# Centring the output weights on chip, one residual update per tile, and the attention denominator as a ninth place of the state product, in a two-layer transformer block with top-1 experts

## What is computed

```
x = x + layernorm(attention(layernorm(x)))
x = x + layernorm(ffn(layernorm(x)))

attention: q, k, v = x @ W + b;  16 heads of 8;  q, k = elu(q) + 1, elu(k) + 1
  s = running sum of k v^T over the tokens of a sequence;  z = running sum of k
  value = (q s) / (q z + 1e-6);  output = values @ Wo + bo
ffn: logits = x @ w_router.T;  the best of 16 experts per token, score = sigmoid(logit)
  out = (silu(x w_gate.T) * (x w_up.T)) @ w_down.T
      + (up * silu(gate)) @ down_proj of the chosen expert, on score * x
layernorm(y) = (y - mean(y)) / sqrt(var(y) + 1e-5), no gain, no offset
```

## Time and profile before

| | |
|---|---|
| time of 3 runs | 351.54 us median, 349.24 to 351.72 |
| the profiled execution | 347.56 us, its span 345.8 us |
| busy, share of the span | PE 264.6 us (77%), DVE 286.4 us (83%), ACT 186.6 us (54%), POOL 192.7 us (56%) |
| granted TensorE clock, mean | 0.913 of 2.4 GHz |
| stage 1 | up to about 154 us of the span |
| stage 2 | up to about 230 us |
| stage 3 | from about 240 us, its last PE product before 325 us |

### The profile page before, as it was taken

How to read it: one execution, slowest core, us unless ns; L and a number is a source line. 1 busy time by engine, 2 the same in 40 slices (tenths; PEclk the granted TensorE clock), 3 DMA queues, 4 the chain that set the end, 5 groups by cost and what they waited for, 6 DMA issues and landing times.

```text
span 345.8 us, 6250 instructions
## 1 busy us (share of the span) xinstructions
PE 264.6 (77%) x1465; PEld 184.2 (53%) x1465; DVE 286.4 (83%) x1138; ACT 186.6 (54%) x572; POOL 192.7 (56%) x221
## 2 busy tenths in 40 slices
PE   3459999999998995638887988821999999999000
PEld 1125556555554553325555655521999889988000
DVE  5998999999999999996998787640379999999930
ACT  2524656565665552257666664203899888885000
POOL 5056777767775863200054556570007888888870
PEclk9988999999999998967999899985899999999655
DMA  6999900000000000000011111126950101110000
GB/s 187 374 426 396 396 4 0 2 3 0 2 0 2 2 0 0 1 1 2 1 62 64 63 62 64 64 100 229 355 166 18 35 31 43 41 36 29 25 2 0
DMA packets 13668, 28.39 MB, mean 82 GB/s; under 512 B 1950, under 2 KB 10150, under 8 KB 12610
## 3 DMA queue, kind: packets, MB, share of 16 engines
q1 hardware_dynamic: 10448, 21.57, 17.1%
q0 software_dynamic: 3040, 6.37, 5.4%
q10 hardware_dynamic: 146, 0.07, 0.1%
HBM read 15.38 MB, written 13.60 MB: 84 GB/s over the span
## 4 chain that ended last, share of the span: by engine, by line
PE 39%; DVE 24%; POOL 18%; issue 12%; DMA 4%; ACT 1%; POOLq 0%; ACTq 0%; SPq 0%; another core or an unknown queue 0%; DVEq 0%
PE banks L1009 13%; POOL out L490 10%; POOL rows L484 6%; PE banks L1028 5%; PE banks L1100 5%; DVE hT L814 2%; PE banks L1037 2%; PE banks L1134 2%; POOL sorted_rows L474 2%; DVE stats L641 2%; DMA rows<-in_x 2%; PE banks L997 2%; DVE num L740 1%; DVE rows L857 1%; DVE stats L849 1%
## 5 line engine op out<-in xcount | busy, mean ns | idle before, releaser
L1009 PE MATMUL banks<-kv,upto 128*128 128x512 f32 x128 | 63.5, 621 | 1.3 <-POOL kv L449 1.3
L449 POOL TENSOR_TENSOR kv<-qk,vv 128x1024 f32<-128x1024 f32 x32 | 62.4, 1950 | 2.5
L1134 PE MATMUL banks<-xsT,w_now 128*128 128x128 f32 x376 | 52.6, 284 | 0.4 <-DVE hT_e L948 0.4
L490 POOL DMA_INDIRECT out<-rows,token_i x47 | 46.8, 997 | 9.8 <-issue 8.2
L443 POOL TENSOR_TENSOR qk<-ex,rl 128x256 f32<-128x256 f32 x32 | 23.3, 727 | 47.0 <-ACT ex L546 47.0
L1134 PEld LDWEIGHTS banks<-xsT,w_now 128*128 128x128 f32 x376 | 47.1, 197 | 1.2 <-issue 0.7
L474 POOL DMA_INDIRECT sorted_rows<-rows,slot_i x32 | 31.7, 992 | 28.7 <-DVE slot_i L804 20.7
L718 DVE TENSOR_TENSOR prod<-banks,qk 128x1024 f32<-128x1024 f32 x32 | 38.9, 1216 | 2.1 <-PE banks L1009 1.5
L740 DVE TENSOR_REDUCE num<-prod 128x128 f32<-128x1024 f32 x32 | 38.7, 1208 | 0.3 <-DVE den L735 0.3
L948 DVE TENSOR_TENSOR hT_e<-silu_e,banks 128x256 f32<-128x256 f32 x47 | 19.4, 412 | 19.8 <-ACT silu_e L623 16.1
L484 POOL TENSOR_TENSOR rows<-rows,yn 128x128 f32<-128x128 f32 x40 | 19.1, 477 | 28.0 <-DVE yn L940 26.1
(11 more groups left out here) (158 smaller groups left out, 640.0 us busy)
## 6 DMA issues: line engine op xcount, KB each, us to landing
sorted_rows<-rows SPq DMA_DIRECT2D x3, 1950.0 KB, 13.3
rows<-sorted_rows SPq DMA_DIRECT2D x11, 520.0 KB, 6.3
w_exp<-in_gate_up SPq DMA_DIRECT2D x4, 1024.0 KB, 19.7
w_exp_down<-in_down SPq DMA_DIRECT2D x4, 512.0 KB, 19.7
rows<-in_x SPq DMA_DIRECT2D x1, 1024.0 KB, 11.1
rows<-in_x SPq DMA_DIRECT2D x1, 768.0 KB, 8.4
out<-rows,token_i POOLq DMA_INDIRECT x47
sorted_rows<-rows,slot_i POOLq DMA_INDIRECT x32
```

Of the source, the lines that this page charges most:

```text
L449: nc.gpsimd.tensor_tensor(kv[:, u, :].rearrange("p (h m d) -> p h m d", h=NH, m=HD), k, v, ALU.mult).then_inc(s_kv, 1)
L490: nc.gpsimd.indirect_dma_start(out=out_rows, out_offset=bass.IndirectOffsetOnAxis(ap=token_i[:, j - 1:j], axis=0), in_=rows[:, j - 1, 0:D] ...
L1009: ins = nc.tensor.matmul(ps_s[u % 2][:, cols], upto[:], kv[:, u, cols], start=True, stop=True)
L1134: ins = nc.tensor.matmul(ps_gue[u % 2][:, c * P:(c + 1) * P], w_now[:, u % 2, c * P:(c + 1) * P], xsT[:, u % 2, :], start=True, stop=True)
```

## The change

Two things are done together.

*Centring.* The last step of both sub-layers is linear, so a mean over the 128 outputs can be taken out of the weights: DVE subtracts from each row of Wo, of the shared w_down, of every expert's down_proj and of bo its mean (`centre_steps`: a sum of the row, then one fused instruction). Then the layernorm of the output needs no offset: x + y * rstd is one fused DVE instruction per tile. In stage 2 ACT's `ya` and DVE's two adds per group go, and four fused instructions come. In stage 3 `yn`, POOL's add and DVE's last adds go, and the norm steps of a quad are 12 in place of 15 (`scale_steps`, 11, which uses that the two half means are opposite, and the token index); the output of tile i is made one quad after its sum, in place of two, and POOL only sends. Wo and bo are centred before the first statistics, w_down in tile 4 of stage 1, the experts' weights after the routing is done.

*Ninth place.* The attention output is laid out place first (the weights are permuted on the host), so that k stands behind the eight products k v of each tile in one array `kvq`, and the sum of k (128 columns) lands right behind the 1024 columns of the state in PSUM. DVE makes one product of 1152 columns and one reduction to 144 values, in place of two of each. PE sums k after the state and not before it, and waits first until v of the next tile has been read. ACT adds epsilon in even tiles. The projection is written to the other parity's banks, and waits for the product of the tile before. In odd tiles DVE adds the carried parts afterwards.

```diff
+def centre_steps(nc, series, rows_of, sums, ready=None):
+    n, width = rows_of.shape[1], rows_of.shape[2]
+    yield series.done(nc.vector.tensor_reduce(sums, rows_of, AX, ALU.add))
+    series.wait()
+    ins = nc.vector.scalar_tensor_tensor(
+        out=rows_of, in0=sums.rearrange("p (n o) -> p n o", o=1).to_broadcast([P, n, width]), scalar=-1.0 / width,
+        in1=rows_of, op0=ALU.mult, op1=ALU.add)
+    yield ins.then_inc(ready, 1) if ready else ins
...
+            for j in range(ST):
+                pool.wait_ge(s_fin, j + 1)
+                nc.gpsimd.indirect_dma_start(
+                    out=out_rows, out_offset=bass.IndirectOffsetOnAxis(ap=token_i[:, j:j + 1], axis=0),
+                    in_=rows[:, j, 0:D], in_offset=None,
+                    bounds_check=NTOK - 1, oob_is_err=False).then_inc(s_out, 16)
...
+                if u % 2 and live(t - 1, NT):
+                    if t == 1:
+                        act.wait_ge(s_eps, 1)
+                    act.wait_ge(s_sums, t)
+                    nc.scalar.activation(den[:, 0, :], sums[:, 0, D:CW], ACT.Identity, bias=eps_den[:]).then_inc(s_den, 1)
...
-                if live(s + 3, NG):
-                    act.wait_ge(s_norm2, s + 4)
-                    for k in range(GT):
-                        c = tiles(GT * (s + 3) + k)
-                        ins = nc.scalar.activation(
-                            ya[:, (u + 1) % 2, k * D:(k + 1) * D], flat(rows[:, c, D:2 * D]),
...
+            centring = Series(dve, s_centre, 0)
+            dve.wait_ge(s_bias, 16)
+            finish(centre_steps(nc, centring, bias[:].rearrange("p (n d) -> p n d", n=1), row_sums[:, 0:1])
+                   ).then_inc(s_centred_o, 1)
+            dve.wait_ge(s_w, 16)
...
-                    dve.wait_ge(s_z, t + 1)
-                    nc.vector.tensor_tensor(zq[:], ps_qkv[u % 2][:, 3 * D:4 * D], qk[:, u, 0:D],
-                                            ALU.mult).then_inc(s_chain, 1)
+                    dve.wait_ge(s_s, t + 1)
+                    at_least(dve, s_sums, t - 1)
+                    nc.vector.tensor_tensor(
+                        prod[:, u % 2, :].rearrange("p (m c) -> p m c", c=D),
+                        ps_s[u % 2].rearrange("p (m c) -> p m c", c=D),
+                        kvq[:, u, Q0:Q0 + D].rearrange("p (o c) -> p o c", o=1).to_broadcast([P, HD + 1, D]),
+                        ALU.mult).then_inc(s_prod, 1)
                     other()
                 if u % 2 == 0 and live(t, NT):
-                    nc.vector.tensor_tensor(carry[:], ps_qkv[0][:, 0:CW], head_mask[:], ALU.mult).then_inc(s_chain, 1)
+                    nc.vector.tensor_tensor(carry[:], ps_qkv[0][:, 0:CW], head_mask[:], ALU.mult).then_inc(s_carry, 1)
                     other()
                 if live(t - 1, NT):
-                    dve.wait_ge(s_chain, CH * (t - 1) + S_READ[1 - u % 2] + 3)
-                    nc.vector.reciprocal(rden[:], rden[:]).then_inc(s_recip, 1)
+                    if u % 2:
+                        dve.wait_ge(s_den, t // 2 + 1)
+                    else:
+                        dve.wait_ge(s_added, t // 2)
+                    nc.vector.reciprocal(rden[:], den[:, 1 - u % 2, :]).then_inc(s_recip, 1)
                     other()
-                if live(t, NT):
-                    dve.wait_ge(s_s, t + 1)
-                    nc.vector.tensor_tensor(
-                        prod[:].rearrange("p (h m d) -> p h m d", h=NH, m=HD),
-                        ps_s[u % 2][:].rearrange("p (h m d) -> p h m d", h=NH, m=HD),
-                        qk[:, u, 0:D].rearrange("p (h o d) -> p h o d", h=NH, o=1).to_broadcast([P, NH, HD, HD]),
-                        ALU.mult).then_inc(s_chain, 1)
-                    other()
-                if live(t - 1, NT):
                     dve.wait_ge(s_recip, t)
-                    dve.wait_ge(s_chain, CH * t)
                     at_least(dve, s_att_t, t - 2)
-                    nc.vector.tensor_tensor(att[:, 1 - u % 2, :].rearrange("p (h m) -> p h m", h=NH),
-                                            num[:].rearrange("p (h m) -> p h m", h=NH),
-                                            rden[:].rearrange("p (h o) -> p h o", o=1).to_broadcast([P, NH, HD]),
+                    nc.vector.tensor_tensor(att[:, 1 - u % 2, :].rearrange("p (m h) -> p m h", h=NH),
+                                            sums[:, 1 - u % 2, 0:D].rearrange("p (m h) -> p m h", h=NH),
+                                            rden[:].rearrange("p (o h) -> p o h", o=1).to_broadcast([P, HD, NH]),
                                             ALU.mult).then_inc(s_att, 1)
                     other()
                 if live(t, NT):
-                    dve.wait_ge(s_chain, CH * t + Z_READ[u % 2])
-                    nc.vector.tensor_reduce(den[:], zq[:].rearrange("p (h d) -> p h d", h=NH), AX,
-                                            ALU.add).then_inc(s_chain, 1)
+                    dve.wait_ge(s_prod, t + 1)
+                    nc.vector.tensor_reduce(sums[:, u % 2, :], prod[:, u % 2, :].rearrange("p (n d) -> p n d", d=HD), AX,
+                                            ALU.add).then_inc(s_sums, 1)
                     other()
-                    dve.wait_ge(s_chain, CH * t + multiplied)
-                    at_least(dve, s_att, t)
-                    nc.vector.tensor_reduce(num[:], prod[:].rearrange("p (n d) -> p n d", d=HD), AX,
-                                            ALU.add).then_inc(s_chain, 1)
-                    other()
-                    dve.wait_ge(s_chain, CH * t + multiplied + 1)
-                    if u % 2 == 0:
-                        nc.vector.tensor_scalar(rden[:], den[:], EPS_DEN, None, ALU.add).then_inc(s_chain, 1)
+                    if u % 2:
+                        dve.wait_ge(s_sums, t + 1)
+                        dve.wait_ge(s_carried, t // 2 + 1)
+                        nc.vector.tensor_tensor(sums[:, 1, 0:D], sums[:, 1, 0:D], ps_xT[:, 2 * D:3 * D], ALU.add)
                         other()
-                    else:
-                        dve.wait_ge(s_carried, t + 1)
-                        nc.vector.scalar_tensor_tensor(out=rden[:], in0=den[:], scalar=EPS_DEN,
+                        nc.vector.scalar_tensor_tensor(out=den[:, 1, :], in0=sums[:, 1, D:CW], scalar=EPS_DEN,
                                                        in1=ps_xT[:, 3 * D:2 * D + CW],
-                                                       op0=ALU.add, op1=ALU.add).then_inc(s_chain, 1)
-                        other()
-                        dve.wait_ge(s_chain, CH * t + multiplied + 2)
-                        nc.vector.tensor_tensor(num[:], num[:], ps_xT[:, 2 * D:3 * D], ALU.add).then_inc(s_chain, 1)
+                                                       op0=ALU.add, op1=ALU.add).then_inc(s_added, 1)
...
-                    for half in range(2):
-                        dve.wait_ge(s_ya, 2 * (s + 2) + 1 + half)
-                        xg = rows[:, tiles(GT * (s + 2) + 2 * half, 2), 0:D]
-                        yield nc.vector.tensor_tensor(
-                            xg, xg, ya[:, u % 2, 2 * half * D:2 * (half + 1) * D].rearrange("p (t d) -> p t d", d=D),
-                            ALU.add).then_inc(s_x1, 1)
-                    dve.wait_ge(s_x1, 2 * (s + 3))
+                    dve.wait_ge(s_norm2, s + 3)
+                    for k in range(GT):
+                        t = GT * (s + 2) + k
+                        x1 = flat(rows[:, tiles(t), 0:D])
+                        yield nc.vector.scalar_tensor_tensor(
+                            out=x1, in0=flat(rows[:, tiles(t), D:2 * D]), scalar=rstd2[:, 1, tiles(t)], in1=x1,
+                            op0=ALU.mult, op1=ALU.add).then_inc(s_x1, 1)
+                    dve.wait_ge(s_x1, GT * (s + 3))
...
+            dve.wait_ge(s_w2, 16)
+            shared = centre_steps(nc, centring, w_d, row_sums[:, 0:FC], s_centred_d)
+            step1(4, 0, shared, 1)
...
+            dve.wait_ge(s_wexp, 16 * (E // 4) * 2)
+            for e in range(0, E, 4):
+                ins = finish(centre_steps(nc, centring, w_exp_down[:, e:e + 4, :, :].rearrange("p e c d -> p (e c) d"),
+                                          row_sums[:, e * FC:(e + 4) * FC]))
+            ins.then_inc(s_centred_e, 1)
...
+            def norm_quad(q, n, norm):
+                c = tiles(4 * q, n)
+                dve.wait_ge(s_stats3, min(4 * (q + 1), ST))
+                yield nc.vector.tensor_scalar(token_i[:, c], rows[:, c, TOKEN], -1.0, float(NTOK), ALU.mult, ALU.add)
+                for ins in scale_steps(nc, norm, [stats3[:, 0:n, k] for k in range(6)], D,
+                                       [scratch3[:, k, 0:n] for k in range(3)], rstd3[:, q % 2, 0:n]):
+                    yield ins
+            def outputs(q, first, last):
+                dve.wait_ge(s_series3, SQ * (q + 1))
+                for i in range(4 * q + first, min(4 * q + last, ST)):
```

(45 more changed lines are left out.)

196 lines of the change are left out of this document (91 added, 105 removed).

## The result

The changed kernel took 367.12 us (median of 4, 365.58 to 370.49) where the kernel before took 350.46 in the same rounds: a ratio of 1.049, with an interval of 1.040 to 1.058. Faster by 13 us was forecast; it is slower by 17. Its profiled execution took 367.04 us, of which 365.2 are its span.

A forecast was written before the change was run, and what follows sets the result against it. PE was taken to set stage 1's period with DVE nearly full, DVE's small steps, PE's down product and the ranks stage 2, POOL stage 3. Terms +0.9 + 2.2 + 0.4 - 1.5 - 2 - 9.0 - 4.2 = -13.2 gave 338.3 us; range 332 to 348.

The forecast's parts named there:

- I take 1.48: Stage 3: 1.48 us a tile in place of 1.68 over 45 tiles, -9.0 us; ends -10.4 and -3.6.
- rival 2: Stage 3 keeps DVE's pace, 1.60 to 1.68 a tile, loop gains only 0 to -3.6: 346 us; chance 20%.
- The tail: After stage 3's last sum: POOL's last transfers end S + 8.8 after last sum S, 13.05 before; -4.2 us.
- Stage 2: DVE's second `hT`, which starts the down product, comes 0.3 earlier in each of seven groups: -2 us, bounds -4 and +1.
- 7.25 a pair: Stage 1, PE: 7.25 against 7.07 us for 12 steady pairs of tiles, +2.2 us; bounds 0 and +4 (7.4).
- rival 1: Stage 1: each `att` waits for POOL's `kv`, up to 1.7 us, making DVE 4.5 a tile: 358 us; chance 7%.
- The ring: Stage 1: projection to `kv` 4.64, then PE's restart, state, sums and transposes: 7.21 us in an even tile, about 7.1 odd.
- +2.0: Start and stage 1 together: the terms +0.9 (start), +2.2 (PE), +0.4 (centring w_down) and -1.5 (last four tiles).
- -1.5: Last four tiles of stage 1: DVE is the bound and gains, partly from the stalled `att`; bounds -3 and +1.
- +0.9: Start: DVE centres bo and Wo before the first statistics, which move from 7.54 to 8.4; +0.9 us.
- Centring the experts: Between the stages: DVE centres experts' weights from 229.8 until 239.4, before its next work at 243.63; 0 us.
- The 0.86 for faster: Whole kernel: 86% chance of faster by over 1%, from 55 + 14 + 17 of case 2's 20.

The follow-up runs named there:

- e4_shifted: Changed kernel plus satisfied waits on ScalarE (ACT) just ahead of stage 3, 31 instructions more; 340.92 us, ratio 0.981.
- e1_centring: Kernel before plus the centring and the outputs of one operation, with its own attention; 337.23 us, ratio 0.972.
- the first four: The runs `e1_centring`, `e2_ninth`, `e3_spaced` and `e4_shifted`, measured on one chip beside the kernel before at 346.71 us; none had a stop.
- e14_held: Centring alone, with POOL waiting for all 47 outputs before it sends the first; 393.44 us, ratio 1.135.
- e16_held_steps: `e14_held` plus SyncE raising a semaphore that nobody waits for 16 times after each expert tile's sum; 393.30 us.
- e2_ninth: Kernel before plus the ninth place of the attention alone; 349.13 us, ratio 1.008.
- e11_side_centring: Centring alone on the attention of before, run again beside the changed kernel on another chip; 361.99 us, ratio 1.036.
- e13_half_rows: Centring alone, with expert up products multiplying only the first 64 of a tile's 128 tokens; 371.82 us.
- e3_spaced: Changed kernel plus a POOL fill of 128 x 512 zeros ahead of each output transfer but the first; 379.42 us, ratio 1.095.
- e10_pool_shifted: Changed kernel plus 64 waits on POOL ahead of its first output transfer; 362.61 us, ratio 1.043.
- e5_again: The changed kernel itself, unchanged, run again; 365.94 us against 349.91, ratio 1.045.
- e8_side_after: The changed kernel unchanged, run beside three other kernels on one chip; 363.85 us against 347.23, ratio 1.042.
- e12_records: Kernel before plus 32 waits for each expert tile's sum on SyncE; 362.20 us, ratio 1.043.
- the two tests of recording: `e12_records`, with added waits on SyncE, 362.20 us, and `e16_held_steps`, with added semaphore steps on SyncE, 393.30 us.

## Why the prediction was wrong

**The step that failed** is one of stage 3: "POOL is left with the indirect DMA, 0.98 and 0.30 between two: 1.29 a tile, below everything else", and with it "I take 1.48". I priced the transfers by POOL's own time and asked only whether POOL would be the bound. That they would come closer together than any the trace of before shows beside working engines cost nothing in my sum, and no rival had it. Where it stops it costs 20 to 23 us of stage 3: 92.12 less 69.1 to 69.2 here, 89.36 less the same at the least. Of the 22.9 us between the changed kernel and `e4_shifted`, 16.0 are idle time of TensorE (18.4 us in that stage for 2.4). The rest goes with its clock. The granted clock fell to the lower level (1.2 GHz) after four of the six stops, for 13.7 us in all. Eight matmuls that take 1.06 at the upper level took 1.83 there:

```profile
281.25 1.83 PE L1165 MATMUL banks<-xsT,w_now 128*128 128x128 f32 x8
```

As an estimate, 13.7 us at half speed cost 6.9. Without the stops the step holds. From 258 to 262 the changed kernel's sums are 1.45 apart, and on the chip without stops stage 3 took 8.4 (`e4_shifted`) and 8.5 us (`e1_centring`) less, where -9.0 was forecast. DVE was not the bound, so rival 2 is out. Its small steps went back to 0.16 once POOL's additions were gone, as the Trainium skill, "SBUF — State Buffer", section "Who interferes with whom", would have it; the trace agrees. The tail, forecast -4.2, gave -3.7 in every kernel with transfers 1.29 apart.

**Stage 2** was forecast at -2. From its first `xmT` to its last the kernel before took 60.35 us. The centring alone took 58.19 without stops, which is the term; it took 63.17 with them, and the changed kernel 63.91. Of the 5.0 between the two runs of the centring, 2.1 lie in the first group, where the clock was low for longer (see between stage 1 and 2). The other groups are then 8.5 apart with single ones of 9.2 to 10.8. Even the kernel before has one such, 10.76, that none of the first four has, so a few stops cost the kernel before some us too. In this stage TensorE's semaphore steps come up to 1.8 us late in every run with an incomplete record, `e14_held` and `e16_held_steps` with their output transfers held back among them. Scatters in fours run there; that they do it was only argued.

**Stage 1** was forecast at 7.25 a pair and bounded by 7.4. It is 7.42 in `e2_ninth`, 7.43 in the changed kernel over tiles 16 to 28. The mechanism was right: PE waits at the state for POOL's product in both tiles of a pair, and `att` is 0.29 as forecast (rival 1 did not come but for one `att` of 2.01). The term was mis-sized, by 0.17 a pair, 2 us. I had costed the odd tile as nearly the even one, and let ACT's added epsilon cost "up to 0.2" at most. The ring of the changed kernel, odd then even:

```profile
125.28 1.96 POOL L492 TENSOR_TENSOR kvq<-kvq,vv 128x1024 f32<-128x1024 f32 x1
125.81 0.81 PE L1056 MATMUL banks<-w_qkvo,xnT 128*128 128x384 f32 x2
125.90 0.31 ACT L562 ACTIVATE den<-sums,eps_den 128x16 f32<-128x16 f32 x1 [0.81 <-DVE sums L768]
...
127.59 1.96 PE L1029 MATMUL banks<-kvq,upto 128*128 128x512 f32 x4
127.70 0.74 POOL L485 TENSOR_TENSOR kvq<-ex,rl 128x256 f32<-128x256 f32 x1 [0.45 <-ACT ex L586]
128.52 1.97 POOL L492 TENSOR_TENSOR kvq<-kvq,vv 128x1024 f32<-128x1024 f32 x1
...
129.62 0.38 PE L1035 MATMUL banks<-kvq,upto 128*128 128x128 f32 x2
...
130.04 1.36 DVE L743 TENSOR_TENSOR prod<-banks,kvq 128x1152 f32<-128x1152 f32 x1 [0.76 <-PE banks L1035]
130.06 0.81 PE L1056 MATMUL banks<-w_qkvo,xnT 128*128 128x384 f32 x2
```

From one projection to the next it is 4.25 us here (4.17 in most pairs) and 3.25 in the other tile. DVE idles 0.76 for PE here, so it isn't the bound.

The ring isn't all that failed in stage 1. The start and stage 1 together had +2.0, and the last `att` is 4.6 late. The projection of tile 24 is 3.5 late (107.74 for 104.26); from there to the last `att` 1.2 more come, where the last four tiles were to give -1.5. That term counted on part of the stalled `att`, which is still there: it begins 0.10 after POOL's product and lasts as long. These are the two rows of the changed kernel, and below them the last `att` before and after the change:

```profile
139.38 1.96 POOL L492 TENSOR_TENSOR kvq<-kvq,vv 128x1024 f32<-128x1024 f32 x1
139.48 2.01 DVE L761 TENSOR_TENSOR att<-sums,rden 128x128 f32<-128x128 f32 x1
...
150.44 0.29 DVE L728 TENSOR_TENSOR att<-num,rden 128x128 f32<-128x128 f32 x1
...
155.08 0.29 DVE L761 TENSOR_TENSOR att<-sums,rden 128x128 f32<-128x128 f32 x1
```

The rest of that difference was not taken apart.

**Between stage 1 and 2** the second `hT` came 7.05 later than before (162.62 and 169.67) where the first came 3.8 later. The granted clock was at the lower level from 148.9 to 159.2 before, and from 151.8 to 168.9 in the changed kernel, with PE busy 21.25 of 30 us (the first window above) and not 24.39. The second up products of the group, before and changed:

```profile
160.94 1.02 PE L1059 MATMUL banks<-xmT,w_ffn 128*128 128x512 f32 x2
...
167.12 1.89 PE L1088 MATMUL banks<-xmT,w_ffn 128*128 128x512 f32 x2
```

`e2_ninth` and `e4_shifted` have it too, `e1_centring` does not (its low stretch ends at 160.4). But the new attention is not what decides. `e11_side_centring` and `e13_half_rows`, with the attention of before, have it (low to 165.7 and 165.5, the second `hT` 4.9 and 4.8 after the first), and `e3_spaced` and `e10_pool_shifted`, with the new one, have less of it (3.0 and 2.5; 5.1 in the changed kernel, 1.8 before). What makes it longer stays open. It is worth some 3 us where it comes, was in no term, and is part of the 63.91 of stage 2 (the first group took 10.11 for 7.57).

**The start** came to +0.4 for +0.9: bo had landed at 6.86 and not 7.33. In `e5_again` and `e8_side_after`, the same kernel, the statistics began at 8.40 and 8.13, so +0.9 was in reach too. Centring the experts was hidden, as forecast: the centring alone has its first sum 1.6 earlier than before.

**The sum, by halves, where nothing stops.** By the medians of the rounds on that chip (346.71 before) the centring gives -9.5 us, the ninth place +2.4, and both with the waits of `e4_shifted` -5.8, ratio 0.981, for a forecast of -13.2. The spans of the profiled executions say -13.9 (331.9 against 345.8), +3.6 and -6.3. The first is to the digit what the centring's terms had forecast (+0.9 + 0.4 - 2 - 9.0 - 4.2). That is luck: the profiled execution of `e1_centring` lies 3.5 under its median, that of `e2_ninth` 2.0 over its own. In the spans the two together are 4 us slower than the sum of both alone; by the medians 1.3, so most of it is which execution was profiled. The changed kernel without those waits was not run on a chip without stops. The 0.86 for faster was also too sure of itself: it held cases for engines and waits only, and none for a resource that the trace of before never shows under more load.

## What to carry to other kernels

When an edit brings a queue's transfers closer together than the trace shows them beside working engines, price that as an unknown with a bound, however idle the issuing engine is, and space them first if the end of the kernel allows. When an effect is gone in an experiment, run the unedited program beside it before believing the edit: four kernels here seemed to have cured what their chip did not have. A time that a theory foretold is no proof of it; look at the rows that its mechanism must change (`e12_records` gave the time and not one stop). A long gap is no stop either until the engine is seen to idle in it (`e13_half_rows` has 21 such gaps and four stops).

## What the runs showed of the hardware

- **TensorE's semaphore steps can come late, though its matmuls don't.** In the stop at 293.9 five semaphore steps of TensorE are due, of matmuls that started from 293.6 to 295.5. All five are recorded from 297.41 to 297.65, in order; the first is 3.5 us after its matmul's end. 16 matmuls lie between the first and the last of them. In every run that stops, 20 to 35 steps of stage 3 are that late (by over 0.5 us), all TensorE's, and none in any other run. So by the records ACT and DVE wait for results that exist. Whether a step or only its recording is held back can't be told from this; ACT started 0.02 after the record.
- **Chips, or hours, differ by 25 us on one program, by 0.5 on another.** `e1_centring` and `e11_side_centring` are the same kernel, 337.23 and 361.99 us. The kernel before took 346.71 and 345.38 on the two chips without a stop, 347.23 to 350.46 on the others. The transfers are no slower where it stops: an output packet of 4096 bytes takes 0.19 us in the median of either run. Where nothing stopped with transfers at 1.29, the trace holds all of the engines' semaphore steps; on the other chips 87 to 97% of them. That is a mark and not shown to be a cause: the kernel before lacks 12% and hardly stops, and 21.2 steps a us were recorded in `e16_held_steps` without a stop. In the two tests of recording the transfers came 1.66 apart or not at all, and every execution here was recorded by the profiler, so a part of the records in the stops, those of the transfers' packets above all, is not ruled out.
- **Spacing counts at 0.2 us.** Transfers of 64 KB 1.29 apart: gaps up to 5.0; 1.53 apart: up to 2.9; 1.66: no late step, but the expert tiles are 1.65 apart there too, and no run has 1.66 with tiles of 1.45 on a chip that stops. What in a transfer holds the steps back (its bytes, its 32 packets, where my expectation had 64, POOL's writing of descriptors) was not tried.
